# One-core language-model tower: band scores, masks, values and value projections in 32x32 and 128x32 matmul tiles

## What is computed

```python
base = (j > i) & (j <= i + W)          # W = 64, i a query of the block, j over 2 * W keys
sc = jnp.einsum('bhnid,bhnjd->bhnij', Qb, Kw) / np.sqrt(D)
p = jax.nn.softmax(jnp.where(mask, sc, -jnp.inf), axis=-1)
out = jnp.einsum('bhnij,bhnjd->bhnid', p, Vw)
```

## Time and profile before

| | |
|---|---|
| median of 3 runs | 3002.09 us (2997.6 to 3002.82) |
| the profiled execution: time | 3003.33 us |
| its span | 3001.5 us |
| PE busy | 2668.5 us (89%), 32904 records |
| PEld busy | 1793.9 us (60%) |
| DVE busy | 1795.5 us (60%) |
| ACT busy | 1091.1 us (36%) |
| POOL busy | 752.9 us (25%) |
| mean granted TensorE clock | 0.971 |

### The profile page before, as it was taken

How to read it: one execution, slowest core, us unless ns; L and a number is a source line. 1 busy time by engine, 2 the same in 40 slices (tenths; PEclk the granted TensorE clock), 3 DMA queues, 4 the chain that set the end, 5 groups by cost and what they waited for, 6 DMA issues and landing times. The chain is left out here.

```text
span 3001.5 us, 83138 instructions
## 1 busy us (share of the span) xinstructions
PE 2668.5 (89%) x32904; PEld 1793.9 (60%) x32904; DVE 1795.5 (60%) x5503; ACT 1091.1 (36%) x1898; POOL 752.9 (25%) x998
## 2 busy tenths in 40 slices
PE   2899899899999899899899994299999999999998
PEld 1566666666666566566666663166656565666666
DVE  4556556556556556566566556775767667675720
ACT  0343343343343343433333431143333434343343
POOL 1011111121121121121121100134444453434543
PEclk9999999999999999999999998599999999999999
DMA  2000000010010010010000001001020211101020
GB/s 71 11 23 24 17 24 23 17 28 18 17 28 18 18 29 16 19 28 16 21 26 16 23 9 45 15 29 59 30 64 28 65 46 49 64 28 61 30 67 29
DMA packets 51568, 93.71 MB, mean 31 GB/s; under 512 B 7980, under 2 KB 36728, under 8 KB 51096
## 3 DMA queue, kind: packets, MB, share of 16 engines
q0 software_dynamic: 18432, 50.36, 5.9%
q1 hardware_dynamic: 32792, 38.52, 3.9%
HBM read 55.29 MB, written 33.55 MB: 30 GB/s over the span
## 5 line engine op out<-in xcount | busy, mean ns | idle before, releaser
L985 PE MATMUL S_ps<-hT,w 128*128 128x512 f32 x1024 | 478.4, 614 | 15.1 <-ACT hT L694 12.1
L998 PE MATMUL O_ps<-w,hid 128*128 128x256 f32 x2048 | 460.3, 379 | 0.0
L496 POOL DMA_INDIRECT rows<-in_tok_table,idx_now x128 | 129.4, 1011 | 1171.5 <-PE M_ps L883 928.0
L998 PEld LDWEIGHTS O_ps<-w,hid 128*128 128x128 f32 x2048 | 383.0, 190 | 62.5 <-issue 15.3
L1096 DVE TENSOR_REDUCE mxL<-S_ps 128x16 f32<-128x2048 f32 x128 | 293.0, 2289 | 155.8 <-PE S_ps L804 155.8
L632 ACT ACTIVATE PT<-S_ps 128x2048 f32<-128x2048 f32 x128 | 240.3, 1878 | 279.0 <-PE S_ps L772 279.0
L705 ACT ACTIVATE hid<-S_ps,b 128x512 f32<-128x512 f32 x256 | 175.3, 687 | 425.4 <-PE S_ps L985 408.5
L985 PEld LDWEIGHTS S_ps<-hT,w 128*128 128x128 f32 x1024 | 190.0, 194 | 223.5 <-issue 212.1
L828 PEld LDWEIGHTS O_ps<-bdV,PT 128*64 128x64 f32 x7680 | 249.2, 138 | 53.4 <-issue 47.5
L665 ACT ACTIVATE bdV<-M_ps 64x256 f32<-64x256 f32 x256 | 98.8, 386 | 490.7 <-PE M_ps L900 489.2
L828 PE MATMUL O_ps<-bdV,PT 128*64 128x34 f32 x7680 | 263.6, 225 | 1.9 <-DVE loc L1112 1.9
(11 more groups left out here) (237 smaller groups left out, 4248.5 us busy)
## 6 DMA issues: line engine op xcount, KB each, us to landing
h_rows<-h SPq DMA_DIRECT2D x64, 256.0 KB, 2.1
w<-in_w SPq DMA_DIRECT2D x16, 1024.0 KB, 5.9
rows<-in_tok_table,idx_now POOLq DMA_INDIRECT x128, 3.5
out_rows<-orow,idx_cur POOLq DMA_INDIRECT x128, 2.4
PT<-in_tables SPq DMA_DIRECT2D x1, 1024.0 KB
b<-in_b SPq DMA_DIRECT2D x8, 128.0 KB, 4.9
hrow<-h_rows,idx_next POOLq DMA_INDIRECT x64
hrow<-h_rows,idx_cur POOLq DMA_INDIRECT x64
```

Of the source, the lines that this page charges most:

```text
L985: mm = nc.tensor.matmul(S_ps[:, m % 2, 0:GT * P], w1[:, c, m * P:(m + 1) * P], hT[g % 2][:, c, :], start=c == 0, stop=c == KC - 1)
L998: mm = nc.tensor.matmul(O_ps[:, q % 2, 0:D], hid[:, m, q * P:(q + 1) * P], w2[:, m, :], start=m == 0, stop=m == FC - 1)
```

## The change

Four things are cut finer, to 32 columns of the array (`QW = 32`, `KW = 96`).

1. Masks: 16 matmuls of 32x32 instead of 8 of 64x64. For the band they have 4 x 96 = 384 columns instead of 512. Each row group needs its tables turned by 0, 32, 64 or 96 partitions, so `latm`, `reach` and `lreach` get copies.
2. Band scores: 32 queries against the 96 keys that they can see, instead of 64 against 128. `Kt` is stored in blocks of 32 keys. VectorE's maximum over `S_ps` reads 1536 columns instead of 2048.
3. Values: 32 queries for each matmul, so 32 columns of weights and four column groups instead of 64 and two. There are twice as many matmuls.
4. Value projections: 32 tokens for each matmul. `bdV`'s partitions now alternate by 32 between even and odd heads. The gates' columns are matmuls of their own. ScalarE's two copies cover all 128 partitions and multiply by 0 or 1 per partition, instead of covering 64 partitions each.

```diff
+QW = 32
+KW = W + QW
...
-        band = sb("band", [P, 2, P], BF16)
-        latm = sb("latm", [P, 2, TS, NL], BF16)
+        band = sb("band", [P, 3, KW], BF16)
+        latm = sb("latm", [P, NG, TS, NL], BF16)
...
-        Kt = [sba(f"Kt{j}", [P, KC, 1 + NB, 2, W]) for j in range(2)]
+        Kt = [sba(f"Kt{j}", [P, KC, 2 * (1 + NB), 2, QW]) for j in range(2)]
...
-        reach = sba("reach", [P, 2 * W], BF16)
-        lreach = sba("lreach", [P, S], BF16)
+        reach = sba("reach", [P, NG, 2 * W], BF16)
+        lreach = sba("lreach", [P, 2, S], BF16)
...
+                v = bank[:, 0:D].rearrange("p (a q d) -> p a q d", a=2, d=HD)
                 for j in range(2):
-                    v = bank[W * j:W * (j + 1), 0:D + 2 * (GW + E)].rearrange("p (a n) -> p a n", a=2)[:, :, 0:D // 2]
-                    nc.scalar.activation(bdV[par][W * j:W * (j + 1), 2 * k:2 * k + 2, :, j, 0:HD],
-                                         v.rearrange("p a (q d) -> p a q d", d=HD), ACT.Copy)
+                    nc.scalar.activation(bdV[par][:, 2 * k:2 * k + 2, :, j, 0:HD], v, ACT.Copy, scale=c_parity[:, 2 + j:3 + j])
...
-            for g in range(0, NG, 2):
-                for a, n, rows_ in ((0, g, 0), (1, g, W), (1, g + 1, 0), (0, g + 1, W)):
-                    nc.tensor.matmul(into(S_ps[W * a:W * (a + 1), n, :]), identb[rows_:rows_ + W, rows_:rows_ + W],
-                                     mask(a, rows_), start=True, stop=False)
+            for n in range(NG):
+                own_ = slice(QW * n, QW * (n + 1))
+                for a in range(NG):
+                    nc.tensor.matmul(into(S_ps[QW * a:QW * (a + 1), n, :]), identb[own_, own_], mask(own_, a, (n - a) % NG),
+                                     start=True, stop=False)
...
-                        for a in range(2):
-                            x = 2 * t + a
-                            into = S_ps[W * a:W * (a + 1), g, D * c:D * (c + 1)].rearrange("p (j a k) -> p a j k", j=2, a=2)
-                            mm = nc.tensor.matmul(into, Qt[par][32 * g:32 * g + 32, c, W * x:W * (x + 1)],
-                                                  Kt[par][32 * g:32 * g + 32, c, x:x + 2, :, :], start=False, stop=c == KC - 1)
+                        for a in range(NG):
+                            x = NG * t + a
+                            into = S_ps[QW * a:QW * (a + 1), g, 2 * KW * c:2 * KW * (c + 1)].rearrange("p (j a k) -> p j a k", j=2, k=QW)
+                            mm = nc.tensor.matmul(into, Qt[par][32 * g:32 * g + 32, c, QW * x:QW * (x + 1)],
+                                                  Kt[par][32 * g:32 * g + 32, c, x:x + 3, :, :].rearrange("p a j k -> p j a k"),
+                                                  start=False, stop=c == KC - 1)
...
-                    for a in range(2):
-                        x = 2 * t + a
+                    for a in range(NG):
+
+                        x, q = 2 * t + a // 2, QW * (a % 2)
...
-                            weights, vals = PT[:, p, x - back, W * back:W * (back + 1)], bdV[par][:, x - back, p, :, :]
+                            weights, vals = PT[:, p, x - back, W * back + q:W * back + q + QW], bdV[par][:, x - back, p, :, :]
...
-                        mm = nc.tensor.matmul(O_ps[W * a:W * (a + 1), t % 2, 2 * OW * p:2 * OW * (p + 1)], weights,
+                        mm = nc.tensor.matmul(O_ps[QW * a:QW * (a + 1), t % 2, 2 * OW * p:2 * OW * (p + 1)], weights,
...
                 for n in range(2):
...
+                        for a in range(NG):
+                            mm = nc.tensor.matmul(bank[QW * a:QW * (a + 1), n * (D // 2):(n + 1) * (D // 2)], lot(c, 2 * n + a // 2),
+                                                  wvg[:, c, slice(*halves[a % 2])], start=c == 0, stop=c == KC - 1)
+                for c in range(KC):
+                    for a in range(NG):
+                        mm = nc.tensor.matmul(bank[QW * a:QW * (a + 1), D:D + GW + E], lot(c, a), wvg[:, c, gates_],
+                                              start=c == 0, stop=c == KC - 1)
...
-                    nc.vector.tensor_reduce(mxL[:, k - 6, :], S_ps[:, :, :].rearrange("p g (h n) -> p (g h) n", n=P),
+                    nc.vector.tensor_reduce(mxL[:, k - 6, :].rearrange("p (g h) -> p g h", g=NG),
+                                            S_ps[:, :, 0:4 * KW].rearrange("p g (h n) -> p g h n", n=KW),
```

More of the change, by code:

```diff
@@ L58, in constants @@
     ident = np.eye(P, dtype=np.float32)
[L59 to L62, removed]
+    near, wide = i[:, None] % QW, np.arange(KW)[None, :]
+    ring = (wide > near) & (wide <= near + W)
+    band = np.stack([np.where(m, 0.0, NEG) for m in (ring & (wide >= W), ring & (wide >= W - QW), ring)], 1)
     tiles = S // P
@@ L65, in constants @@
     lat = np.where(np.arange(NL)[None, None, :] <= tok // (S // NL), 0.0, NEG)
-    parity = np.stack([(i // HD) % 2 == 0, (i // HD) % 2 == 1], 1)
+    parity = np.stack([(i // n) % 2 == j for n in (HD, QW) for j in range(2)], 1)
     own = (i[:, None] // HD == np.arange(LH)[None, :]) * (NL / S)
@@ L69, in constants @@
     lane = np.broadcast_to(i[None, :], (P, P))
-    reach = np.tile(np.concatenate([np.where(k[:, None] <= k[None, :], 0.0, NEG), np.where(k[None, :] < k[:, None], 0.0, NEG)], 1), (2, 1))
+    key = (QW * (i // W) + i % QW)[:, None]
+    reach = np.concatenate([np.where(key <= k[None, :], 0.0, NEG), np.where(k[None, :] < key, 0.0, NEG)], 1)
     lreach = np.tile(np.where(np.arange(NL)[:, None] <= np.arange(S)[None, :] // (S // NL), 0.0, NEG), (2, 1))
-    pick = np.zeros((P, KC + 1, 2, W))
+    pick, lpick = np.zeros((P, KC, 2, 2, QW)), np.zeros((P, 2, NL))
     for g in range(NG):
-        for c in range(KC + 1):
-            for j in range(2):
-                pick[32 * g + PIECES * (2 * c + j):32 * g + PIECES * (2 * c + j + 1), c, j, :] = 1.0
+        for j in range(2):
+            for c in range(KC):
+                pick[32 * g + PIECES * (2 * c + j):32 * g + PIECES * (2 * c + j + 1), c, :, j, :] = 1.0
+            lpick[32 * g + PIECES * (2 * KC + j):32 * g + PIECES * (2 * KC + j + 1), j, :] = 1.0
+    pick = np.concatenate([pick.reshape(P, -1), lpick.reshape(P, -1)], 1)
+    turned = lambda a, n: np.stack([np.roll(a, QW * g, 0) for g in range(n)], 1)
     f = lambda a: np.ascontiguousarray(a.reshape(P, -1).astype(np.float32))
-    cols = [f(ident), f(parity), f(own), f(i), f(band), f(lat), f(np.roll(lat, W, 0)), f(before), f(lane), f(reach), f(lreach), f(pick)]
+    cols = [f(ident), f(parity), f(own), f(i), f(band), f(turned(lat, NG)), f(before), f(lane), f(turned(reach, NG)), f(turned(lreach, 2)), f(pick)]
     digit = np.arange(1, RADIX, dtype=np.int64)[None, :] << (32 - BITS * (1 + np.arange(DIGITS, dtype=np.int64)))[:, None]
@@ L654, in act_item @@
                 for j in range(2):
[L655 removed]
+                    ins_ = nc.scalar.activation(Kt[par][:, k, 2:, j, :], bank[:, :].rearrange("p (a k) -> p a k", k=QW),
                                                 ACT.Copy, scale=c_parity[:, j:j + 1])
@@ L746, in pe_scores @@
                 stand(pe)
-                pe_masks(pe, lambda x: x, lambda a, rows_: lreach[rows_:rows_ + W, :])
+                pe_masks(pe, lambda x: x, lambda rows_, a, turn: lreach[rows_, turn % 2, :])
                 for g in range(NG):
@@ L759, in pe_scores @@
                 pe_masks(pe, lambda x: x.rearrange("p (b n) -> p b n", n=P),
-                         lambda a, rows_: reach[rows_:rows_ + W, :].unsqueeze(1).to_broadcast([W, NB // 2, P]))
+                         lambda rows_, a, turn: reach[rows_, turn, :].unsqueeze(1).to_broadcast([QW, NB // 2, P]))
                 for later in range(2):
@@ L1361, in _ @@
             for par in range(2):
-                nc.vector.memset(Kt[par][:, :, 0, :, :], 0.0)
+                nc.vector.memset(Kt[par][:, :, 0:2, :, :], 0.0)
                 chain(dve, nc.vector.memset(bdV[par][:, :, :, :, :], 0.0))
-                nc.vector.memset(bdV[par][0:W, :, :, 0, HD:OW], 1.0)
-                nc.vector.memset(bdV[par][W:P, :, :, 1, HD:OW], 1.0)
+                for a in range(NG):
+                    nc.vector.memset(bdV[par][QW * a:QW * (a + 1), :, :, a % 2, HD:OW], 1.0)
                 chain(dve, nc.vector.memset(bdL[par][:, :, :, :], 0.0))
```

42 lines of the change are left out of this document (17 added, 25 removed).

## The result

The changed kernel takes **3214.63 us** (median of 4 runs, 3214.22 to 3221.68) against 3002.45 of the kernel before beside it: ratio 1.0714, 95% interval 1.0695 to 1.0734. I had forecast 2829 and a range up to 2920, so the sign is wrong, and 386 us lie between forecast and result.

What follows compares the result with a forecast made beforehand. Attention, 32 iterations, was taken as bound by PE's matmuls; 32 x 5.6 = 179 us saved, less 5 at the start, gives 174, so 3003.3 becomes 2829 us; forecast 2800 to 2850, full range 2778 to 2920.

Steps and rivals of the forecast that it cites:

- rival C: Instruction supply: value tasks want 19.6 KB in 1.36 us against 16.4 KB in 1.2; 2845 to 2895 us, chance 0.10.
- the sum of 5.6 us an iteration: Attention iteration: 4.6 us saved from `S` 5 to its end plus 1.0 in `S` 0 to 4, of PE's 7.2.
- full clock but for two slices: Profile before: PE at full clock except two slices, the choice for the first expert, which the change doesn't touch.
- Masks: `S` 0 to 5: sixteen 32x32 tiles in one wave take a mask from 0.56 to 0.36 us, 0.2 less.
- Band scores: `S` 6 to 9: a task goes from 1.60 to 1.08 us, 0.52 less.
- four waves each: Band scores: 32 records in waves of 8 before, 64 in waves of 16 after; a wave 0.22 us, then 0.16.
- Values: `O` 0 to 3: 40 rounds of 34 ns take a task from 2.35 to 1.36 us, 0.99 less, four times.
- rivals A: Values don't gain: a round stays at 59 ns, only masks and bands gain; 2919 us, chance 0.11.
- Rival B: Only two column streams run, so 32-column tiles go in pairs and a projection bank takes 2.01 us; 3174 us, chance 0.11.
- the rule that the prediction held against itself: Values: weight loads overlap matmuls in flight only when row groups differ, so a round takes 60 ns and values gain nothing.
- Projections: Value projections: 1184 against 1184 columns per column group, 1.01 us a bank, no gain if four streams run.
- VectorE's new waits: Ahead of `S` 6, 7 and 8: 1.6 us an iteration of PE's savings turn into waits for VectorE's maximum.

Runs made afterwards that it cites:

- order_after: The changed kernel with `O` 0 and `O` 1 moved ahead of `K` 1 and `PV`: 3242.0 us; its own before, the earlier kernel so reordered, took 3058.92.

## Why the prediction was wrong

**The step that failed first is the price of rival C.** It took the time of a packet, 1.2 us, for the period in which instructions arrive, and concluded "about the limit"; the sum of 5.6 us an iteration has no term for the supply at all. The packet's own time is 1.1 us still; the period is 3.5. Put right, the rival's own line says it all: 320 instructions want 1.36 us and get 256 in 3.5. A stall was priced at 0.2 to 1.0 us a value task, half of it hidden, 0.4 to 2 us an iteration; measured are 8.3 us an iteration. The rows above show 0.82, 2.44, 2.14 and 0.92 us of gaps in 20 us, and only the first and third of them fall in a value task: what a value task uses up, the tasks behind it lack. The mechanism was named and given 0.10. The traces before could have warned: there a value task has 80 matmuls and 80 loads in 2.35 us, 68 a us, just under the 73.

The Trainium skill, "Runtime: NRT & Kernel Launch", section "Instruction fetch mechanics", has the block of 256 instructions in 16 KiB, and the fetch of the next while one executes; the count of 160 packets agrees. It calls the cost of a block's boundary mostly hidden. That holds in the kernel before; in the kernel after, with 264 us of new gaps, it does not. Its warning that a taken branch stalls the fetch has its rows in both kernels (26.6 and 29.5 us, six times each).

**Not priced at all: the clock behind a gap.** I read "full clock but for two slices" as a property of the attention. By the means, the span has 2 x (1 - 0.919) x 3213 = 520 us at half clock after and 2 x 0.029 x 3001.5 = 174 before. If PE worked through all of the 346 us more, its work would have taken half the time at full clock: up to 173 us.

**Masks**: 0.36 us as predicted; 0.18 in the band (1061.22 to 1061.40), where I had 0.16 to 0.25. Right.

**Band scores**: wrong. Predicted 1.05 - 0.22 + 0.10 = 0.93 us with four waves of sixteen; measured 1.26, slower than the 1.05 of half as many, wider records. A band-score task as a whole (`S` 7, 1061.22 to 1062.66) takes 1.44 us in place of 1.08, over the 1.3 that the prediction had set as its own sign of being wrong. The step "four waves each" failed: sixteen tiles at once came about with bf16 matmuls and with f32 ones not.

**Values**: 34 ns a round, right to a nanosecond where there is no gap, so rivals A and B fall, and with A the rule that the prediction held against itself, 60 ns a round. A whole task saved less, 0.85 us for `O` 0 in place of 0.99: the prediction took 2.35 us for a task from the spacing of its records, not from start to next start, which is 12.24 - 9.57 = 2.67 in the same rows. **Projections**: 1.04 us a bank against 1.01, right. **Maximum**: 1758 ns against 1.75 us, right. **VectorE's new waits**: wrong, 51 us more were predicted and 34 fewer came; PE, starved, arrives later than the maximum.

**The balance**, rough: 264 us of gaps, up to 173 of clock, (1.44 - 1.08) x 4 x 32 = 46 for the band scores, less 51 + 34 = 85 of waits for the maxima that didn't come: 398, where 386 are to be explained. The clock's share is an upper bound and no run separates it from the gaps, so that the two sums nearly meet is no proof of it. The one hint is order_after: 10 us more of gaps beside its own before than the kernel after has, some 105 us less at half clock, and a loss smaller by 29 us.

Rival B's 3174 us lay near the result for the wrong reason: its test, a projection bank of 2.0 us, even came true in the slow stretches. Only the clock beside it and the bank of 1.04 us at full clock tell the two apart.

## What to carry over

Count PE's instructions, loads and f32 halves included, per microsecond of every task, and not only their columns: above 73 a us for longer than a block, a smaller tile buys idle time, and behind the longer gaps here came half clock as well. A quiet stretch ahead lends a block or so and no more, so cut fine only tasks with such a stretch before them (masks everywhere and `O` 0: 2938.86 us, 2% below the kernel before). And where a resource is asked whether it is the limit, the distance from start to start is its price, not the length of one transfer.

## What the runs showed of the hardware that I had not expected

- Short of instructions, PE gets 256 in 3.46 to 4.28 us, and a gap ends some 2.5 us after the start of the last fetch.
- Behind an idle time of 2.44 us the granted clock stood at 0.50 for six us of full work; behind one of 2.14 us it fell to 0.50 some 2 us later (windows above).
- Sixteen bf16 tiles of 32x32 run at once (64 matmuls of 384 columns in four groups of sixteen, 1.25 us at the lower clock by their length), while 64 f32 records of 192 columns took 1.26 us at full clock, where four waves would be 0.65.
- The same fine task changed the whole by -11 us (`O` 0) or +39 us (`O` 3), by its place alone.
